# A sort by one-hot matmuls: VectorE's comparisons read their iota from PSUM, and layer 0's transform has five staging buffers

## The reference

```python
# first part: three relational layers, weights[l] is (9, 128, 128)
out = x
for l in range(3):
    X = jnp.einsum('ne,ref->rnf', out, weights[l])
    msg = X[edge_type, dst] + biases[l][edge_type]      # edge_index[1] is dst
    hidden = jax.ops.segment_sum(msg, src, num_segments=N)
    out = jax.nn.relu(hidden) if l + 1 < 3 else hidden
x = layernorm(x + out)
# second part: attention over the edges and a loop at each node
alpha = beta * cosine(x[row], x[col])                   # row is src, col is dst
alpha = softmax of alpha over the edges of one row
x = layernorm(x + segment_sum(alpha * x[col], row))
```

## Time and profile before

| | |
|---|---|
| median of 3 runs | 5676.5 us (5673.23 to 5679.72) |
| profiled execution, its own time | 5667.57 us |
| span of its profile | 5665.5 us |
| mean granted clock of TensorE | 0.723 |
| busy, share of the span | PE 55%, PEld 35%, DVE 43%, ACT 15%, POOL 48% |

### The profile page before, as it was taken

How to read it: one execution, slowest core, us unless ns; L and a number is a source line. 1 busy time by engine, 2 the same in 40 slices (tenths; PEclk the granted TensorE clock), 3 DMA queues, 4 the chain that set the end, 5 groups by cost and what they waited for, 6 DMA issues and landing times.

```text
span 5665.5 us, 68647 instructions
## 1 busy us (share of the span) xinstructions
PE 3123.5 (55%) x13926; PEld 2003.1 (35%) x13927; DVE 2460.1 (43%) x9525; ACT 858.2 (15%) x1992; POOL 2704.9 (48%) x2839
## 2 busy tenths in 40 slices
PE   7112996555555555655555455556555533333698
PEld 4001553333333333333333333333333333322476
DVE  9101885333333333533333333334333322222699
ACT  2002991100010010000010001000001000000365
POOL 1774004555555555255555555552555566666100
PEclk9555997777777777877767777777777755555799
DMA  4000001222222222612212222216212121111454
GB/s 146 3 1 3 0 0 32 56 61 52 52 63 54 52 55 62 135 48 57 52 52 63 53 53 58 61 51 138 51 50 57 48 69 43 43 42 43 100 190 155
DMA packets 447303, 340.20 MB, mean 60 GB/s; under 512 B 263666, under 2 KB 404522, under 8 KB 447112
## 3 DMA queue, kind: packets, MB, share of 16 engines
q0 software_dynamic: 90368, 165.49, 12.5%
q1 hardware_dynamic: 153512, 113.25, 6.5%
q10 hardware_dynamic: 203360, 60.73, 4.4%
HBM read 232.12 MB, written 107.13 MB: 60 GB/s over the span
## 4 chain that ended last, share of the span: by engine, by line
another core or an unknown queue 41%; PE 18%; issue 16%; DVE 12%; DMA 5%; ACT 4%; DVEq 4%; ACTq 1%; POOL 0%; SPq 0%; POOLq 0%
PE ps L931 6%; PE ps L961 4%; PE ps L952 3%; DVE region L547 3%; DMA edge_absent<-region 2%; DVE oh L464 2%; DVEq L290 2%; DMA edge_counts<-region 2%; PE ps L1000 2%; PE ps L1028 2%; ACT ps L1077 1%; ACT region L1088 1%; DVE region L479 1%; DVE region L350 1%
## 5 line engine op out<-in xcount | busy, mean ns | idle before, releaser
L860 POOL DMA_INDIRECT region<-x_of_type,pair x2520 | 2399.8, 952 | 2365.9 <-PE ps L952 1035.6
L952 PE MATMUL ps<-oh,region 128*128 128x102 f32 x5040 | 1197.8, 342 | 1580.7 <-DVE region L547 1440.7
L961 PE MATMUL ps<-region 128*128 128x510 f16 x4200 | 1607.8, 461 | 536.2 <-issue 407.3
L952 PEld LDWEIGHTS ps<-oh,region 128*128 128x128 f32 x5040 | 1166.7, 256 | 2080.9 <-DVE region L547 1579.0
L464 DVE TENSOR_SCALAR oh<-iota_w,pair 128x102 f32<-128x102 f32 x2528 | 701.2, 278 | 2608.6 <-remote 1718.8
L961 PEld LDWEIGHTS ps<-region 128*128 128x128 f16 x4200 | 494.0, 124 | 779.7 <-issue 767.6
L547 DVE TENSOR_TENSOR region<-region,ps 128x102 f32 x2520 | 647.7, 257 | 13.5 <-issue 13.4
L1088 ACT COPY region<-ps 128x510 f32<-128x510 f32 x155 | 89.8, 580 | 3405.6 <-remote 1974.8
L931 PE MATMUL ps<-region 128*128 128x420 f16 x2016 | 392.4, 356 | 322.8 <-issue 259.4
L842 POOL DMA_INDIRECT scattered_edges<-region x304 | 300.6, 989 | 209.4 <-DVE ends L408 109.2
L931 PEld LDWEIGHTS ps<-region 128*128 128x128 f16 x2016 | 196.7, 99 | 519.0 <-issue 310.0
(11 more groups left out here) (179 smaller groups left out, 1546.2 us busy)
## 6 DMA issues: line engine op xcount, KB each, us to landing
region<-x_of_type,pair POOLq DMA_INDIRECT x2520
edge_counts<-region ACTq DMA_DIRECT2D x155, 255.0 KB
arrays<-edge_counts SPq DMA_DIRECT2D x40, 960.0 KB, 4.8
x_of_type<-region SPq DMA_DIRECT2D x50, 576.0 KB, 7.0
edge_absent<-region ACTq DMA_DIRECT2D x155, 127.5 KB
region<-edge_absent SPq DMA_DIRECT2D x40, 480.0 KB
x_of_type<-x0st SPq DMA_DIRECT2D x51, 192.0 KB
scattered_edges<-region POOLq DMA_INDIRECT x304
```

Of the source, the lines that this page charges most:

```text
L860: pool.indirect_dma_start(out=grow[:, u % GR, :], out_offset=None, in_=xt, in_offset=bass.IndirectOffsetOnAxis(ap=idx[:, u % GR:u % GR + 1 ...
L952: pe.matmul(ps[:, 6 + n % 2, t * RB:(t + 1) * RB], grow[:, u % GR, :], oh[:, u % U, 0:RB], start=True, stop=True).then_inc(s_used, 1)
L961: mm = pe.matmul(ps[:, c, 0:CW], cl[:, q % CR, c * P:(c + 1) * P], cr[:, q % CR, :], start=False, stop=False, skip_group_check=True)
```

## The change

Three things are changed.

1. An iota of 840 float16 numbers is put into PSUM bank 7. GpSimd makes `steps_down` (128 x 896, float16: 128 b + partition in block b), and TensorE turns its 7 blocks with transposes into the bank behind the transform (`turn_steps`, semaphore `s_ln`). The two comparisons of the sort read `sort_iota` there and not `iota_s` in SBUF.
2. `take_few` adds 16 zeros that lie in the same bank (`sort_zero`, cleared by VectorE before the first use) where it copied before, so that it too has an operand in PSUM. VectorE waits for `s_ln` before the clearing.
3. X0 goes from 6 to 5, so `x0st` has three buffers. The extra iota moves GpSimd's count of set-up steps on by one, for which VectorE and TensorE wait.

```diff
-X0 = 6
+X0 = 5
...
+        steps_down = sb("steps_down", [P, -(-NT // P) * P], F16)
...
+        SORT_N = -(-NT // P)
+        sort_iota = ps[:, 7, 0:NT // 2].bitcast(F16)
+        sort_zero = ps[:, 7, SORT_N * P // 2:SORT_N * P // 2 + KR * 4]
...
-            dve.wait_ge(s_pool, 12)
+            dve.wait_ge(s_pool, 13)
...
             def take_few(h, t):
-                nc_.tensor_copy(few[:, h, :], cols[:, bass.ds(t * 4, KR * 4)]).then_inc(s_few, 1)
-
+                nc_.tensor_tensor(few[:, h, :], cols[:, bass.ds(t * 4, KR * 4)], sort_zero, ALU.add).then_inc(s_few, 1)
+
+            dve.wait_ge(s_ln, 1)
+            step(nc_.memset(sort_zero, 0.0))
             take_few(0, 0)
...
-                    nc_.tensor_scalar(hot_q[:, k, :], iota_s[:, 0:P], q, None, ALU.is_equal).then_inc(s_hot, 1)
-                    nc_.tensor_scalar(oh_s[:, k, :], iota_s, s, None, ALU.is_equal).then_inc(s_cell, 1)
+                    nc_.tensor_scalar(hot_q[:, k, :], sort_iota[:, 0:P], q, None, ALU.is_equal).then_inc(s_hot, 1)
+                    nc_.tensor_scalar(oh_s[:, k, :], sort_iota, s, None, ALU.is_equal).then_inc(s_cell, 1)
...
+            nc_.iota(steps_down[:, :].rearrange("p (b m) -> p b m", m=P), pattern=[[P, -(-NT // P)], [0, P]], base=0,
+                     channel_multiplier=1, allow_small_or_imprecise_dtypes=True).then_inc(s_pool, 1)
...
+            def turn_steps(bank, at, n):
+                for b in range(n):
+                    mm = pe.transpose(ps[:, bank, at + b * P // 2:at + (b + 1) * P // 2].bitcast(BF16),
+                                      steps_down[:, b * P:(b + 1) * P].bitcast(BF16), diag[:, P:2 * P])
+                mm.then_inc(s_ln, 1)
...
             pe.wait_ge(s_x0e, NB * XC)
+            turn_steps(7, 0, SORT_N)
             pe.wait_ge(s_d, marks["past"])
```

More of the change, by code:

```diff
@@ L219, in gnn_program @@
         ps = ctx.enter_context(nc.psum_tensor("ps", [P, 8, 512], F32))
+        SORT_N = -(-NT // P)
+        sort_iota = ps[:, 7, 0:NT // 2].bitcast(F16)
+        sort_zero = ps[:, 7, SORT_N * P // 2:SORT_N * P // 2 + KR * 4]
+        assert SORT_N * P // 2 + KR * 4 <= 512
         s_edges = sem("s_edges")
@@ L268, in gnn_program @@
         s_sh = sem("s_sh")
+        s_ln = sem("s_ln")
         s_cl = [sem(f"s_cl{u}") for u in range(3)]
@@ L825, in _ @@
                      allow_small_or_imprecise_dtypes=True).then_inc(s_pool, 1)
-            pool.wait_ge(s_pool, 7)
+            nc_.iota(steps_down[:, :].rearrange("p (b m) -> p b m", m=P), pattern=[[P, -(-NT // P)], [0, P]], base=0,
+                     channel_multiplier=1, allow_small_or_imprecise_dtypes=True).then_inc(s_pool, 1)
+            pool.wait_ge(s_pool, 8)
             nc_.affine_select(out=ident[:, :], in_=ident[:, :], compare_op=ALU.not_equal, fill=1.0, base=0,
@@ L831, in _ @@
                               pattern=[[1, P]], channel_multiplier=-1).then_inc(s_pool, 1)
-            pool.wait_ge(s_pool, 9)
+            pool.wait_ge(s_pool, 10)
             nc_.tensor_scalar(negi[:, :], ident[:, :], -1.0, None, ALU.mult).then_inc(s_pool, 1)
             nc_.tensor_copy(diag[:, P:2 * P], ident[:, :]).then_inc(s_pool, 1)
-            pool.wait_ge(s_pool, 11)
+            pool.wait_ge(s_pool, 12)
             pool.sem_inc(s_pool, 1)
@@ L867, in _ @@
         def _(pe):
-            pe.wait_ge(s_pool, 12)
+            pe.wait_ge(s_pool, 13)
             pe.wait_ge(s_const, 112)
+            def turn_steps(bank, at, n):
[3 more added lines that the diff above has]
+                mm.then_inc(s_ln, 1)
             def count_edges():
```

## The result

The changed kernel takes 5712.25 us (median of 4 runs, 5705.94 to 5723.19) where the kernel before takes 5674.86 on the same chip (4 runs): ratio 1.0067, 95% interval 1.005 to 1.0085. It is slower by 37 us; forecast was 5677, with "nothing that can be told" as the likeliest case. Its profiled execution took 5705.94 us, with a span of 5704.0 and a mean clock of 0.723. In a later set of runs, in which the kernel before takes 5782.81 us, the same kernel gave 5810.87, ratio 1.0051, interval 1.0037 to 1.0065.

What follows compares the result with a forecast made beforehand. TensorE was taken to bound the sort after the scatter (0.718 us a column), its late increments the stretch during it. All terms cost 0 but one column, 0.7 us: 5676.5 + 0.7 = 5677; range 5664 to 5748.

Steps and rivals of the forecast that it cites:

- nothing that can be told: Whole kernel: time indistinguishable from no change, within about 0.2% (11 us); own range 5666 to 5688; chance 0.70.
- Thin cover: Sort after the scatter: VectorE takes 0.74 to 0.87 us a column and becomes the bound, +10 to +71 us; chance 0.12.
- The crawl stays: Sort during GpSimd's scatter: about one column per 10.5 us, 36 columns done, release still at 541.2 us; cost 0.
- Freed port: Sort during the scatter: PSUM operands avoid VectorE's port shared with GpSimd, ending the slow stretch; 341 us less, 5336; chance 0.10.
- one in some 10 us: Sort during the scatter: until the indirect DMAs' effect has run off, TensorE's increments arrive one per some 10 us.
- The second part: Sort after the release, 468 columns: VectorE's 0.67 to 0.71 us a column stays under TensorE's 0.718; cost 0.
- fixed part 0.07 between starts: VectorE's sort comparisons from PSUM: each adds 0.07 us between starts besides its elements, giving 0.51 long and 0.14 short.
- The halving: VectorE's 16-bit reads from PSUM: half the 32-bit time per element, 0.52 ns against 1.04.
- the bound (0.15 between starts): VectorE's comparisons after the release: with 0.15 us fixed between starts, 0.87 us a column, costing 71 us.
- Seven transposes and their increment: Before the sort: transposes hidden, at most 2.8 us; VectorE's wait for s_ln costs one column, 0.7 us, bound 2 us.
- the 185 us: Sort's start: a first comparison later than some 185 us would show the forecast wrong.
- Iota chain and five staging buffers: Set-up and transform: one more GpSimd fill, cost 0, uncovered 0.9 us; five pieces still cover a transfer, cost 0.

Runs made afterwards that it cites:

- the two part changes: Changed kernel with its long comparison reading SBUF again, ratio 1.0012; changed kernel with only its long comparison reading PSUM, ratio 1.0027; both against the kernel before.

## Why the prediction was right and where it was wrong

The range (5664 to 5748) held the time, but the likeliest case, nothing that can be told (0.70), did not come. "Thin cover" (0.12) did: VectorE at 0.74 to 0.87 us a column, 11 to 71 us slower; it became 0.775 and 37.

- *The crawl stays.* Right, in effect and in the reading of who waits for what. The release is at 541.11 and four columns go at once, as on every crawling chip with 304 indirect DMAs (541.1 to 542.4 in seven traces); with 200 of them it comes at 392. The wait is for TensorE's increments, of work that is done: VectorE starts 24 or 25 ns behind each whose event the trace has. "Freed port" is refuted by this, and by the gaps, which are still 10 to 11 us with VectorE's operands in PSUM. The detail "one in some 10 us" was wrong: it is one matmul per 2.6 to 2.8 us. What holds the increments back stays open, and so does why one chip has none of it.
- *The second part.* The step that failed is the term "fixed part 0.07 between starts". The halving was right: (648 - 277)/(840 - 128) = 0.52 ns an element, as I carried it over. The fixed part between starts is 0.57 - 0.44 = 0.13 for the long comparison and 0.19 - 0.07 = 0.12 for the short one, where I had taken 0.07 from 32-bit reads of 420 elements. Twice 0.05 to 0.06 turned 0.67 into 0.78, past TensorE's 0.718. The better row was at hand. In the earlier trace rows the same two comparisons, from SBUF, take 0.51 us together; 968 elements at 0.25 ns are 0.24 of it, so 0.27 is left, 0.13 for each instruction. The fixed part is that of this comparison, wherever its operand lies. With it the prediction's sum would have been 968 x 0.52 ns + 0.27 + 0.02 = 0.79 us, above 0.718, and "thin cover" the likeliest case. The 0.07 came from comparable-looking 32-bit reads; no run shows why those start closer together. The margin between 0.71 and 0.718 was too small to be worth 0.70 in any case. That the range held the time is owed to the bound (0.15 between starts) and to "thin cover", not to the sum.
- The rule of the Trainium skill that I set beside it ("VectorE: DVE Perf Modes", "Why PSUM operands drop a tier"), two results per cycle for 16-bit operands in PSUM, is borne out by the 0.52 ns, half of the 32-bit read's 1.04. It is a rule of the slope and could not warn of the fixed part.
- *Seven transposes and their increment.* The price (one column, with three beats or 2 us as the bound) was nearly right, but the timing behind it was not, so this is in part luck. The increment was to arrive one beat after 157.51, at 168, hidden; it came at 176.37, 19 us after the first of seven transposes, since each of the seven counts as a step. VectorE's first comparison started at 176.99 here (174.5 before), at 194.6 in the second profile of this kernel, and at 191.8 and 183.5 in the two part changes; two of the four are past the 185 us that the prediction called a sign of being wrong, because the transform's evictions ended later there. The crawl got 33 or 34 columns done instead of 36: two or three columns, about 2 us. It is cheap because little hangs on the crawl's start, at one column per 10 to 11 us.
- *Iota chain and five staging buffers.* Nothing, as forecast. The buffers alone gave 0.9987, with an interval that touches 1; the iota chain was not run alone, but the scatter starts at 114.54 as before (114.56).

The sum as it should have been: 468 x 0.06 + 2 x 0.78 = 30 us, which is what the loop's end shows. The measured 37 (28 in the later runs) differs from it by amounts for which I have no cause.

Open: what the change does on the chip without a crawl. With a start near 163, as an estimate, and the crawling chips' 0.776 a column, the loop would end near 163 + 503 x 0.776 = 553, and the scatter, which ends last there now, near 546: 7 to 10 us slower, an estimate and not run.

## What to carry to other kernels

Where an engine is to be slowed under the cover of another, work out the margin per step and compare it with the uncertainty of the *fixed* part of each instruction, counted by starts: two instructions a step with 0.05 us each were the whole margin here. Take the fixed part from rows of the very instruction, even with its operand elsewhere, before one of another kind with its operand in the right place. Before tuning for a wait with an unseen releaser, look at the semaphore's own events, and whether another chip has it at all; moving columns from GpSimd to TensorE gained 1.3% on a chip with the wait (200 left) and cost 3.9% on one without it (40 left).

## What was unexpected of the hardware

- The same program takes 5675, 5693 or 5783 us on crawling chips and 4283 on another. During GpSimd's indirect DMAs the sort goes at one column per 10.5 or 11.2 us or at one per 0.716. That is some 330 us; most of the rest lies in the layers (first to last L547): 4383 us in the kernel before, where L464 has 1718.8 us of idleness with an unseen releaser, and 3333 in the kernel with eight matmuls on the other chip, where it has none.
- On the crawling chips TensorE's increments come as if it did one matmul or transpose per 2.6 to 2.8 us during indirect DMAs, of 128 columns or of 420. At the release the increments of four columns come within 0.2 us (541.14 to 541.32 in the kernel before).
- Each indirect DMA holds the crawl for 1.40 to 1.43 us (304, 200 and 12 of them), though GpSimd issues one per 1.32 us in the scatter, so the release comes 27 and 21 us after the last issue there, and 3 us after it in the gather of 12.
- A 16-bit comparison with its first operand in PSUM: 0.52 ns an element, from SBUF 0.25, and from either 0.12 to 0.14 us between starts besides; 840 elements take 648 ns and 434.
- On the chip without the crawl VectorE and GpSimd seem to hold each other a little. With two matmuls a column the long comparison takes 525 ns and GpSimd's DMA 960 on average, with eight 434 and 1156 (groups by line, during the loop). Who yields changed with the rhythm of the loop; why, no run shows.
